# Query and key rows of an attention kernel in transfers of four heads of a row instead of eight

## The chip, the cores and the metric

The kernel runs on one core of a Trainium2 chip. The metric is the device time of one execution in microseconds (us). Matmuls run on TensorE (PE), the other arithmetic on VectorE (DVE), ScalarE (ACT) and GpSimd (POOL); SyncE (SP) computes nothing here, it issues nearly all direct transfers (DMA), in the order of its program, and 16 DMA engines carry them out.

## The reference

32 sequences of 128 tokens with 128 features go through two layers. Layer 0 is a cross-attention with 16 heads of 8 features and then a mixture of 8 experts of which one is chosen; layer 1 is the same attention, masked to be causal, and then 8 experts of which two are chosen. Cut to the parts that the change touches:

```python
x = x + attention0(layernorm(x), ctx, ctx)       # queries from x, keys and values from ctx
x = x + experts0(layernorm(x))
x = x + attention1(layernorm(x), ctx, ctx)       # causal
x = x + experts1(layernorm(x))
# attention: Q, K, V projections + biases, per head of 8 features
scores = einsum('bhqd,bhkd->bhqk', Q, K) / sqrt(8)
out = einsum('bhqk,bhkd->bhqd', softmax(scores), V) @ Wo + bo
```

## The kernel before

The 32 sequences are worked on in eight groups of four (`G = 4`, `GT = 512` tokens). The program has these stages, one after the other, with a barrier of all engines between them except inside the last:

- `prepare`: weights are loaded and turned.
- `project`: for each group n the context rows and the x rows are loaded (lines 406 and 408), x is normalised (statistics on DVE, line 338), both are transposed, and queries of layer 0 and keys of both layers are computed. Each query or key is split into three bf16 parts whose sum is the fp32 value (ACT line 489, DVE 520, ACT 494, POOL 548) and stored to the scratch tensors `q_parts` and `k_parts` in HBM (line 232, three stores of 384 KB for each group, in rows of 1 KB). The part tiles have two buffers, so that the parts of group n wait for the stores of group n-2.
- attention 0: scores from the parts, softmax, product with the values, output projection.
- `experts0`: the layer 0 experts, and the queries of layer 1, which are stored in the same way.
- attention 1 with the layer 1 experts and the final sum behind it, in one block.

In HBM, one row (a part and a feature of the head) of a group holds 16 heads x 512 tokens in bf16. `load_side` (line 228 of the profile) brings one side, query or key, of one group into a tile `qq` or `kk`: partitions 0 to 47 take the first eight heads of each row, partitions 64 to 111 the other eight, 8 heads x 512 tokens x 2 bytes = 8 KB for each partition, side by side. The rows of the three parts go to six slots of eight partitions, some of them twice, in runs of 3, 2 and 1 parts (`RUNS`, `K_RUNS`). One side of a group is so six transfers: three runs x two halves, of 24, 16 and 8 partitions, 192, 128 and 64 KB. `QK_IN` is what the semaphore counts for both sides of a group.

There are three buffers of each tile. The loads stand here in SP's program:

- `project`: after the stores of groups 2, 3 and 4 come both sides of groups 0, 1 and 2 of layer 0 (`early`). The loop body on SP is: load context and x of group n+3, store the parts of group n, and for n = 2, 3, 4 `early(n - 2)`.
- attention 0 and 1: both sides of groups 3 to 7, each when the scores of the group that had the buffer are done (`on_sync`).
- `experts0`: the keys of groups 0, 1, 2 of layer 1 at the start, ahead of the layer 1 weights (lines 1168 to 1172); the queries of these groups each between a store of queries and three fills of `sorted_in` (line 1177).

The readers are TensorE's matmuls of lines 666 (scores) and 687 (scores transposed); scores run three sequences ahead of the rest.

Of the kernel before, what the change touches and what calls it, by code (L numbers as in the profile page):

```python
# [17 lines left out]
DH = D // H  # L18
# [8 lines left out]
RUNS = ((0, 0, 3), (3, 0, 2), (5, 0, 1))  # L27
# [2 lines left out]
HALF = 64  # L30
AHEAD = 3
QK_BUFS = 3
QK_IN = 16 * 2 * 2 * len(RUNS)
STORED = 16
C4 = 4
NC = H // C4
# [12 lines left out]
def earlier(count):  # L49

    return max(count, 0) if isinstance(count, int) else count
# [94 lines left out]
def build(nc, a, out):  # L146
# [16 lines left out]
    with ctx:  # L163
# [57 lines left out]
        def load_side(eng, l, g, side, signal):  # L221

            tile, src, runs = (qq, q_parts[g], RUNS) if side == "q" else (kk, k_parts[l][g], K_RUNS)
            for slot, part, count in runs:
                by_half = src[part:part + count].rearrange("c d (a i) t -> a (c d) i t", a=2)
                for s in range(2):
                    row = s * HALF + slot * DH
                    eng.dma_start(tile[g % QK_BUFS][row:row + count * DH], by_half[s]).then_inc(signal, 16)

        def store_parts(eng, to, tile, signal):  # L230

# [145 lines left out]
        def project():  # L377
# [7 lines left out]
            with ExitStack() as own, nc.Block() as block:  # L385
# [16 lines left out]
                @block.sync  # L402
                def _(sp):
                    def load(g):
                        sp.wait_ge(c_turned, earlier(g.n - 1))
                        sp.dma_start(c_g[g.p][:], rows(a["ctx_1024"], g)).then_inc(c_in[g.p], 16)
                        sp.wait_ge(ln.stats_s, earlier(g.n - 1))
                        sp.dma_start(x_of(g), rows(a["x"], g)).then_inc(x_in[g.p], 16)

                    def store(g):  # L410
                        for i, (_, _, to) in enumerate(items):
                            sp.wait_ge(part2, g.n * 3 + i + 1)
                            store_parts(sp, to[g.n], parts[g.p][i], kq_out[g.p][i])

                    def early(g):
                        for i, side in ((0, "k"), (2, "q")):
                            sp.wait_ge(kq_out[g % 2][i], STORED * (g // 2 + 1))
                            load_side(sp, 0, g, side, early_in[0])

                    load(FIRST)  # L420
                    load(FIRST.after())
                    load(FIRST.after().after())

                    for n in range(NG):
                        if n + 3 < NG:
                            load(Group((n + 3) // 2, (n + 3) % 2))
                        store(Group(n // 2, n % 2))
                        if n >= 2 and n - 2 < QK_BUFS:
                            early(n - 2)
                    for s in kq_out[0] + kq_out[1]:  # L430
                        sp.wait_ge(s, STORED * (NG // 2))
# [133 lines left out]
        def attention(l, own):  # L565
# [66 lines left out]
            def on_sync(sp):  # L632
                def load(g):
                    sp.wait_ge(st_ps, (g - QK_BUFS + 1) * G * PAIRS)
                    for side in "kq":
                        load_side(sp, l, g, side, qk_in[g % QK_BUFS])

                for g in range(QK_BUFS, NG):
                    load(g)
                for g in range(NG - QK_BUFS, NG):  # L640
                    sp.wait_ge(qk_in[g % QK_BUFS], g // QK_BUFS * QK_IN)

            def on_tensor(pe):
# [8 lines left out]
                def scores(n, u):  # L652

                    buf, t = columns(n)
                    if u == 0 and n % G == 0:
                        if n // G < QK_BUFS:
                            pe.wait_ge(early_in[l], QK_BUFS * QK_IN)
                        else:
                            pe.wait_ge(qk_in[buf], n // G // QK_BUFS * QK_IN)
                    pe.wait_ge(max_s, earlier(n * PAIRS + u - (n < AHEAD)))  # L660
# [467 lines left out]
        def experts0():  # L1128
# [9 lines left out]
            with ExitStack() as own, nc.Block() as block:  # L1138
# [19 lines left out]
                def _(sp):  # L1158
# [4 lines left out]
                    def early(g):  # L1163
                        sp.wait_ge(q_out[g % 2], STORED * (g // 2 + 1))
                        load_side(sp, 1, g, "q", early_in[1])
# [581 lines left out]
```

## Time and profile before

| | |
|---|---|
| median of 3 runs | 824.84 us (823.54 to 827.07) |
| the profiled execution's own time | 818.21 us |
| its span, first to last instruction | 816.4 us |
| PE / DVE / ACT / POOL busy | 77% / 59% / 48% / 44% of the span |
| bytes moved by DMA | 87.56 MB in 59708 packets |
| `project` (to the first score matmul) | until 114.6 us of the span |
| attention 0 | 114.6 to about 266 us |
| `experts0` | about 266 to 404 us |
| attention 1 | 404 to about 625 us |
| layer 1 experts, sum | to the end |

Durations of instructions come from the profiled execution, whose own time is 6.6 us below the median of the three runs; its span leaves out 1.8 us around the first and last instruction. In the rows below, SPq is the queue of SP: the time shown there is the time that SP needs to issue a transfer, with what it has to wait for room ahead of it, not the time of the transfer. "DMA share" is the mean busy share of the 16 DMA engines.

### The profile page before, as it was taken

Reading aid. Unit: us, or ns where it says so; the run is one execution under the profiler, and the core shown is the slowest. Engines: PE = TensorE matmul, PEld = TensorE weight load, DVE = VectorE, ACT = ScalarE, POOL = GpSimd, SP = SyncE. Lnnn points to the kernel's source line nnn. Section 1 sums busy time; section 2 is a strip of 40 time slices with the busy share of each in tenths; the row PEclk is TensorE's granted clock in tenths of the full one; section 3 lists DMA queues with packets and bytes.
Section 4 is the critical chain, followed back from the end, with each engine's and each line's share of the span. In section 5 each row is a group of like instructions: output and inputs, shape, how many; then the busy total and the mean of one; then the engine's idle time right before and its main releaser. Section 6 shows DMA issues by size and latency. Waiting matters only on the chain. (4 is left out here: it accounts for less than half of the span.)

```text
span 816.4 us, 22712 instructions
## 1 busy us (share of the span) xinstructions
PE 626.6 (77%) x8205; PEld 478.1 (59%) x8205; DVE 482.4 (59%) x1255; ACT 392.5 (48%) x900; POOL 359.6 (44%) x555
## 2 busy tenths in 40 slices
PE   1574549979998589999389988888740799999980
PEld 1353327757676344544166765666530799999980
DVE  1462356757773367675266789888725355555545
ACT  0684426757776234444135766566730344444440
POOL 5384350101000325352324467777886255555550
PEclk9996768999999699999569999999955799999995
DMA  3389831635400875587604444320011222222218
GB/s 83 113 239 193 208 138 32 111 70 101 87 3 2 137 229 232 172 228 249 255 2 80 79 89 99 76 55 26 25 44 46 54 67 62 65 63 64 68 33 312
DMA packets 59708, 87.56 MB, mean 107 GB/s; under 512 B 8904, under 2 KB 50128, under 8 KB 56528
## 3 DMA queue, kind: packets, MB, share of 16 engines
q1 hardware_dynamic: 51024, 75.03, 35.8%
q0 software_dynamic: 4352, 8.99, 3.5%
q10 hardware_dynamic: 4224, 2.10, 0.9%
q8 instruction: 68, 1.11, 0.6%
q14 instruction: 40, 0.33, 0.1%
HBM read 43.99 MB, written 41.96 MB: 105 GB/s over the span
## 5 line engine op out<-in xcount | busy, mean ns | idle before, releaser
L893 DVE TENSOR_REDUCE nm<-bank 128x8 f32<-128x1024 f32 x128 | 155.8, 1222 | 50.3 <-PE bank L666 48.4
L796 ACT ACTIVATE pr<-bank 128x512 f32<-128x512 f32 x256 | 147.1, 603 | 77.1 <-PE bank L690 74.6
L1515 PE MATMUL bank<-exxt,qq 128*128 128x128 f32 (+1 forms) x864 | 109.1, 277 | 0.9 <-ACT exxt L1553 0.7
L1515 PEld LDWEIGHTS bank<-exxt,qq 128*128 128x128 f32 (+1 forms) x864 | 101.2, 185 | 1.4 <-ACT exxt L1553 1.1
L1062 POOL TENSOR_SCALAR_AFFINE_SELECT pr<-pr 128x1024 f32<-128x1024 f32 x64 | 69.7, 1089 | 64.5 <-ACT pr L796 63.9
L705 PE MATMUL bank<-pr,values 128*9 128x128 f32 x2048 | 82.2, 279 | 3.5 <-POOL pr L1062 2.0
L1489 POOL DMA_INDIRECT results<-exy,exre x72 | 71.4, 991 | 29.7 <-issue 29.4
L687 PE MATMUL bank<-qq,kk 48*128 48x128 bf16 x1024 | 76.7, 223 | 3.8 <-ACT pr L796 2.6
L690 PE MATMUL bank<-mt,pick 64*128 64x128 bf16 x1024 | 76.7, 223 | 0.1
L1337 PE MATMUL bank<-e0ch,expert_w 128*128 128x512 f32 x128 | 70.3, 632 | 6.5 <-DVE e0ch L1259 6.5
L1589 DVE TENSOR_TENSOR exhi<-bank,exsi 128x384 f32<-128x384 f32 x72 | 40.1, 557 | 55.1 <-PE bank L1515 37.6
L666 PE MATMUL bank<-kk,qq 48*128 48x128 bf16 x1024 | 55.2, 232 | 19.2 <-PEq L157 7.9
L1092 POOL DMA_INDIRECT sorted_in<-rrrow,rrpli x64 | 63.4, 991 | 14.2 <-issue 14.2
L1523 PE MATMUL bank<-down_w,exhi 128*128 (+1 forms) x432 | 60.1, 275 | 0.1
L666 PEld LDWEIGHTS bank<-kk,qq 48*128 48x128 bf16 x1024 | 37.9, 101 | 37.8 <-issue 19.4
L1566 ACT ACTIVATE exy<-bank,exsh 128x128 f32<-128x128 f32 x72 | 26.5, 368 | 67.5 <-PE bank L1523 43.4
L1069 POOL CAST mp<-nm 128x16 bf16<-128x16 f32 x32 | 6.3, 198 | 119.1 <-DVE nm L893 116.0
L687 PEld LDWEIGHTS bank<-qq,kk 48*128 48x128 bf16 x1024 | 51.7, 98 | 9.4 <-ACT pr L796 5.0
L705 PEld LDWEIGHTS bank<-pr,values 128*9 128x9 f32 x2048 | 43.9, 91 | 17.7 <-issue 4.1
L1523 PEld LDWEIGHTS bank<-down_w,exhi 128*128 128x128 f32 (+1 forms) x432 | 53.9, 191 | 0.3 <-issue 0.3
L1259 DVE TENSOR_TENSOR e0ch<-bank,e0xt 128x512 f32<-128x512 f32 x64 | 42.8, 680 | 17.5 <-PE bank L1328 17.5
L690 PEld LDWEIGHTS bank<-mt,pick 64*128 64x128 bf16 x1024 | 52.3, 98 | 0.3 <-issue 0.3
(208 smaller groups left out, 1168.2 us busy)
## 6 DMA issues: line engine op xcount, KB each, us to landing
sorted_in<-values SPq DMA_DIRECT2D x25, 715.0 KB, 6.4
k_parts<-pj_parts SPq DMA_DIRECT2D x16, 384.0 KB, 3.8
kk<-k_parts SPq DMA_DIRECT2D x32, 192.0 KB
qq<-q_parts SPq DMA_DIRECT2D x32, 192.0 KB
exx<-sorted_in SPq DMA_DIRECT2D x72, 65.0 KB
kk<-k_parts SPq DMA_DIRECT2D x32, 128.0 KB
qq<-q_parts SPq DMA_DIRECT2D x32, 128.0 KB
q_parts<-pj_parts SPq DMA_DIRECT2D x8, 384.0 KB, 3.9
```

The lines of the kernel that those rows point to most:

```text
L666: mm = pe.matmul(s_pair[:, (a * C4 + j) * T:(a * C4 + j + 1) * T], qq[buf][half(a, PROD), u * C4 + j, t], kk[buf][half(a, PROD), u * C4 + ...
L687: pe.matmul(to[a][:, j * T:(j + 1) * T], kk[buf][half(a, PROD), u * C4 + j, t], qq[buf][half(a, PROD), u * C4 + j, t], start=True, stop=Fa ...
L690: mm = pe.matmul(to[a][:, j * T:(j + 1) * T], pick[half(a, HALF), u * C4 + j, :], max_t[n % 3][half(a, HALF), :], start=False, stop=True, ...
L705: mm = pe.matmul(o_bank[32 * j:32 * j + VW, c * T:(c + 1) * T], values[l][:, n, c % 2 * H2 + c // 2 * C4 + j, :], probs[c][:, j * T:(j + 1 ...
L796: act.activation(probs[c], st_bank[(n * NC + c) % ST][:], ACT.Exp, scale=scale).then_inc(exp_s, 1)
L893: dve.tensor_reduce(neg_max[n % 2][:, u * 2 * C4:(u + 1) * 2 * C4], score_banks(n, u).rearrange("q (h k) -> q h k", k=T), AX_X, ALU.max, n ...
L1062: pool.affine_select(out=probs_pair[u][:], in_=probs_pair[u][:], compare_op=ALU.is_ge, fill=0.0, base=0, pattern=[[0, 2 * C4], [1, T]], ch ...
L1092: pool.indirect_dma_start(sorted_in[:], bass.IndirectOffsetOnAxis(ap=place_i[bt.p][:, k, b:b + 1], axis=0), row[bt.p][:, k, b, :], None).t ...
L1337: pe.matmul(y_bank[:], expert0_w[:, e, :], chosen[e % 2][:], start=(e == 0), stop=(e == E - 1)).then_inc(y_ps, 1)
L1489: pool.indirect_dma_start(results[:], bass.IndirectOffsetOnAxis(ap=result[q.g.p][:, q.b:q.b + 1], axis=0), y_g[q.p][:], None).then_inc(y_o ...
L1515: mm = pe.matmul(to[q.p][0:fn, f * T:(f + 1) * T], own_w[q.p][:, w0 + f0:w0 + f0 + fn], x, start=True, stop=True)
L1523: mm = pe.matmul(y_bank[q.p][:, 0:D], hidden[q.p][0:fn, f * T:(f + 1) * T], down_w[0:fn, bass.ds(e, 1), f, :].rearrange("f e d -> f (e d)" ...
```

## The change

Each half row of eight heads goes in two transfers of four heads. A transfer still has the same 24, 16 or 8 partitions, but takes 4 KB for each partition, so it is 96, 64 or 32 KB. One side of a group is twelve transfers instead of six, and all 32 sides together are 384 transfers instead of 192. The two pieces of a half are issued one behind the other. The bytes, their places in HBM and in SBUF, and the place of the loads in SP's program stay as they are; the count that the readers wait for doubles.

```diff
-QK_IN = 16 * 2 * 2 * len(RUNS)
+QK_IN = 16 * 2 * 2 * 2 * len(RUNS)
...
                 for s in range(2):
                     row = s * HALF + slot * DH
-                    eng.dma_start(tile[g % QK_BUFS][row:row + count * DH], by_half[s]).then_inc(signal, 16)
+                    for u in range(2):
+                        heads = slice(u * C4, (u + 1) * C4)
+                        eng.dma_start(tile[g % QK_BUFS][row:row + count * DH, heads], by_half[s][:, heads]).then_inc(signal, 16)
```

## Rows read from the trace of the kernel before

**Rows 1.** The page: the span, DMA busy tenths in 40 slices, the hardware queue.

```profile
span 816.4 us, 22712 instructions
...
DMA  3389831635400875587604444320011222222218
...
q1 hardware_dynamic: 51024, 75.03, 35.8%
```

**Rows 2.** Waits within 57 to 115 us: engine, line, releaser: total, times, longest.

```profile
DVE pj_ln_stats L338 <- DMA x_res<-x: 25.1, 2, 13.1
```

**Rows 3.** Timeline of SP's queue in `project`: start, us, line, operation.

```profile
55.45 2.50 SPq L228 DMA_DIRECT2D kk<-k_parts  x6
58.00 2.25 SPq L228 DMA_DIRECT2D qq<-q_parts  x6
...
64.16 2.63 SPq L232 DMA_DIRECT2D q_parts<-pj_parts  x1
66.84 5.86 SPq L228 DMA_DIRECT2D kk<-k_parts  x6
72.74 2.53 SPq L228 DMA_DIRECT2D qq<-q_parts  x6
...
75.75 0.51 SPq L408 DMA_DIRECT2D x_res<-x  x1
...
84.94 5.10 SPq L228 DMA_DIRECT2D kk<-k_parts  x6
90.08 2.25 SPq L228 DMA_DIRECT2D qq<-q_parts  x6
93.77 1.49 SPq L232 DMA_DIRECT2D k_parts<-pj_parts  x2
```

**Rows 4.** Timeline of DVE and ACT, same stretch, with the idle time before.

```profile
72.14 0.87 DVE L338 BATCH_NORM_STATS2 pj_ln_stats<-x_res 128x6 f32<-128x128 f32 x4 [12.01 <-DMA x_res<-x]
...
89.68 0.87 DVE L338 BATCH_NORM_STATS2 pj_ln_stats<-x_res 128x6 f32<-128x128 f32 x4 [13.10 <-DMA x_res<-x]
...
105.11 0.69 ACT L489 ACTIVATE pj_parts<-bank,bk 128x512 bf16<-128x512 f32 x1 [0.27 <-DMA k_parts<-pj_parts]
```

**Rows 5.** Windows: stretch, length, engines' busy time, PE clock, DMA share, GB/s.

```profile
54.00:57.00 3.00, 2.80 (x10) 1.61 (x11) 1.24 (x8) 2.28 (x5) 3.00 (x5) 1.00 1.00 349
...
74.40:86.80 12.40, 7.43 (x26) 4.54 (x26) 2.18 (x4) 6.22 (x12) 5.19 (x6) 0.67 0.97 168
...
139.00:152.00 13.00, 12.57 (x272) 9.36 (x274) 9.74 (x16) 9.46 (x23) 1.45 (x7) 1.00 0.69 124
148.00:151.00 3.00, 2.86 (x82) 2.04 (x71) 2.36 (x5) 1.97 (x5) 0.06 (x1) 1.00 0.51 82
799.00:804.00 5.00, 0.00 (x0) 0.00 (x0) 2.79 (x5) 0.00 (x0) 0.00 (x0) 0.50 1.00 397
```

**Rows 6.** A load in attention 0: SP's queue, first reader, DMA packets within 139:152.

```profile
138.38 2.28 SPq L228 DMA_DIRECT2D kk<-k_parts  x6
140.71 2.25 SPq L228 DMA_DIRECT2D qq<-q_parts  x6
...
160.79 0.40 PE L666 MATMUL bank<-kk,qq 48*128 48x128 bf16 x8
...
DMA packets 338, 1.61 MB, mean 124 GB/s; under 512 B 144, under 2 KB 144, under 8 KB 144
```

**Rows 7.** SP's queue in `experts0`: the early loads and what follows them.

```profile
266.52 6.86 SPq L228 DMA_DIRECT2D kk<-k_parts  x18
...
296.39 1.33 SPq L1177 DMA_DIRECT2D sorted_in<-values  x1
...
306.53 0.37 SPq L232 DMA_DIRECT2D q_parts<-e0parts  x1
...
337.54 2.09 SPq L1177 DMA_DIRECT2D sorted_in<-values  x3
348.66 0.38 SPq L232 DMA_DIRECT2D q_parts<-e0parts  x1
```

## Prediction

> **What bounds the kernel now.** I read the page first, then the waits and the timelines of the stages that contain the changed loads, then windows over the DMA queues. On the page, see that DMA is no bound of the whole, 36% of the 16 engines' time, but that its load comes in heaps: nearly all engines are busy in slices 4 and 5 of 40 and again around slice 20 [rows 1]. Those early slices are the last part of `project`. There DVE, which wants the x rows of groups 6 and 7, sits idle twice, 25.1 us together [rows 2], and the timeline shows each time the same cause: the x rows arrive at 72.1 and at 89.7 us, 12.0 and 13.1 us after DVE was ready [rows 4]. SP issues those x rows behind a load of queries and keys [rows 3], and the DMA engines are full all the while, a share of 0.97 from 74.4 to 86.8 us [rows 5]. So for some 35 us this stage goes at the pace of the DMA queues, and three of the changed loads lie inside it.
>
> How the three lie on the path: x of group 6 is queued behind the first load, x of group 7 behind the second. The interval between the two arrivals is 17.5 us [rows 4]. In it move one load, 0.52 MB of context and x, and three stores of 0.39 MB; the last two, 1.70 MB, take 4.9 us at the 349 GB/s that the stores reached [rows 5], which leaves 12.6 us for the load. The third load stands ahead of the stores of group 5, and ACT waited for one of these at 105.1 us for 0.27 us [rows 4], behind 15.4 us of computation since 89.7 us. So a longer first, second or third load each moves the end of the stage one for one; shorter ones count for the first two only, the third has 0.27 us to give.
>
> **A load in detail.** The clean case stands in attention 0. Both sides of a group are 1.57 MB, and with 139 to 152 us at 124 GB/s [rows 5] that is the whole of one load, about 12.5 us. SP needed 4.53 us to issue the twelve transfers, 0.38 us each, and the first reader came 22.4 us after the first issue [rows 6]. Of the packets 144 are small, the marks that engines write at the end of a transfer: twelve for each on the mean [rows 6]. That fits 12, 16 and 8 engines for the transfers of 24, 16 and 8 partitions, and then the busiest eight engines carry 2 + 1 + 1 rows for a half, 16 rows of 8 KB for a load. In the last 3 us about eight engines are still at work, share 0.51, 82 GB/s [rows 5].
>
> An engine at work in the load moves 124 / (0.69 x 16) = 11.2 GB/s, so an 8 KB packet takes 730 ns, and 16 of them 11.7 us, nearly the whole load. Packets can be faster: 1 KB stores run at 349 / 16 = 21.8 GB/s, 47 ns a packet, and loads with 4 KB packets over all partitions at 397 / 16 = 24.8 GB/s, 165 ns [rows 5]. These two give a fixed 8 ns and 0.038 ns a byte, so 323 ns for an 8 KB packet and 330 ns for two of 4 KB. The load therefore takes 12.5 us where its busiest engines would need 16 x 0.323 = 5.2 us. What the other 7.3 us are decides this case: shared bandwidth (stays), a cost for each transfer (doubles), or a handicap of big packets (goes).
>
> The Trainium skill (SBUF — State Buffer, section on the DMA port swizzle) says that a transfer's rate goes by the SBUF ports its partitions reach, that partitions 0 to 63 reach only half of the 16 and that each gives 27.2 GB/s. By that rule the 7.3 us are port sharing: four-head pieces land in the same partitions, and the load keeps its time. The trace agrees in direction: the 128-partition loads reach 397 GB/s, these 124, and 82 at their end [rows 5].
>
> **The change part by part.** (1) SP's issues. A load goes from 12 to 24 issues, 4.5 to 9.1 us at 0.38 us each. In `project` this is covered: SP was at work from 55.4 to 92.3 us, but mostly blocked. The first issue of a load and the stores ahead of it took 2 to 4 us each instead of 0.4 [rows 3]; without the blocking a 17.5 us cycle holds 24 x 0.38 + five others of 0.4 = 11.1 us of issuing, so 6.4 us are spare. The order in the queue is unchanged, and as long as the engines have work queued, a later issue moves nothing. If this cover is gone (engines drained before SP comes), the load takes the pace of the issues. The third load ends its issues at about 97 instead of 92.3 us, and the stores of group 5, issued at 93.8 [rows 3], go out 4 us later, still before the engines finish that load at about 102 us (89.7 us, some 2 us of stores, one load less its first packets on the free engines). Cost 0.
>
> (2) The packets on the busiest engines: 16 more times 8 ns, 0.13 us a load.
>
> (3) The marks: 12 more for each load. Below, nothing: the 4 KB loads ran at share 1.00 through about four ends of transfers [rows 5], so an end leaves hardly a gap. Above, the whole unexplained 7.3 us, 0.61 us for each transfer. I take 0.05 us, near the lower end because that row is of the same queue and direction: 0.6 us a load.
>
> (4) The order within a load: the two pieces of one half follow each other, so engines stay on the same partitions for two packets, and an engine that runs ahead has a smaller packet to run ahead with. Halves overlapping is what keeps more than one set of partitions filling. I bound it by -1 and +2 us and take 0.3 us.
>
> Sum for a load 1.0 us; three on the path of `project`, 3.0 us.
>
> (5) The loads of attention 0 and 1: first issue to first reader is 22.4 us [rows 6], and no less in the nine others. The load occupies 13 of them and would occupy 14, or 20.3 us with the upper bound of (3). Cost 0; TensorE's wait stays met beforehand.
>
> (6) `experts0`. The keys take 36 issues instead of 18, 6.9 us more; the weights and the first fill go out later, the fill done at 297.7 us, and the next store waits for POOL until 306.5 us: 8.8 us of cover [rows 7]. If it were short, the stores of queries would slip, and with their two buffers ACT. Each load of queries adds six issues, 2.4 us, and SP is idle for 9.0 us behind the fills [rows 7]. Cost 0.
>
> **The sum.** 818.2 us for the profiled execution becomes 821.2 us. That execution is 6.6 us below the median of the runs, so for the median 824.8 + 3 = 827.8 us. About 0.5%, 4.1 us, is what a measurement of this kernel can tell from no change.
>
> **Rivals.**
>
> *Port-bound and nothing else.* The 7.3 us are bandwidth of the shared partitions, and marks and packets hide under it: 0 to +1 us, 825 us. For it: the lower rate with fewer partitions. Against: an engine between two packets leaves its share to others only if they share its partitions. Chance 0.17.
>
> *A cost for each transfer.* The excess of 7.3 us comes with the twelve transfers, 0.61 us each, and doubles: up to 7.3 us for each of three loads, +22 us, 847 us; a third of it gives 832 us. It decides from 0.11 us a transfer on, where the sum passes 4 us. For it: the 12.5 us nobody accounts for, and that all transfers but a few are under 200 KB. Against: 4 KB packets at share 1.00 through the ends of transfers [rows 5]. Chance 0.18. The Trainium skill (DMA: Bandwidth & Descriptors, Rules for kernel authors) speaks against this change here: it advises to coalesce and says that under 64 KB one pays mostly overhead; a third of the transfers fall to 32 KB. By its measured table a transfer has a floor of 0.68 us, and 12 of them for each of three loads would be an estimated +24 us. No run here shows that floor between overlapping transfers.
>
> *Big packets were the handicap (the other side).* 4 KB packets go at their own 165 ns even in these partitions, since requests of different engines alternate sooner. Then the engines need 5.3 us, and SP's issues become the pace: the 17.5 us cycle falls to SP's 11.1 us, -6.4 us, and the first load from 12.5 to 9.1 us, -3.4 us; the third gives 0.3 us. Together -10 us, 815 us. It decides where a load gets 2.1 us shorter. For it: 730 ns against 323. Against: the same bytes reach the same partitions. Chance 0.15.
>
> *My forecast*, +1 to +6 us: chance 0.50, of which a third lies above 4.1 us.
>
> **The numbers.** Faster 0.15; same 0.17 + 0.34 = 0.51; slower 0.16 + 0.18 = 0.34. The range 819 to 838 us leaves out the strong half of the gain (0.07) and the costs above 0.36 us a transfer (0.08); my likeliest case alone is 825.8 to 831 us.
>
> **What would show it.** The x rows arrive for DVE at about 73 and 92 us instead of 72.1 and 89.7, and the score matmuls begin at 117.6 instead of 114.6 us. A load alone in attention 0 has 384 packets of 4 KB and 288 marks, lasts 13.5 us, and the DMA share in it stays near 0.69 with the rate near 120 GB/s. SP issues 24 transfers in about 9.1 us. From the first score matmul on nothing is longer. Wrong would be: a load of 9 to 10 us paced by SP's issues (rival with small packets), a load of 15 us or more (cost of transfers), a TensorE wait ahead of a group's first line 666, or a `project` in which DVE no longer waits for x.

## The result, and the profile after

The changed kernel takes 811.68 us (809.55 to 812.49, 4 runs) against 824.19 us (822.76 to 827.07, 4 runs) for the kernel before beside it: a ratio of 0.984, 95% interval 0.981 to 0.987. It is 12.5 us faster where the forecast was 3 us slower, and lies below the forecast range of 819 to 838 us. Some later pairs put the kernel before at 821 to 823 us and the changed one at 811.0 us (ratio 0.9845), so the gain is 11 to 12.5 us. The profiled execution of the changed kernel took 809.55 us, 8.7 us below that of the kernel before.

The page of the changed kernel, which answers to [rows 1]:

```profile
span 807.8 us, 22904 instructions
...
DMA  3379941433301764576503334400011222222209
...
q1 hardware_dynamic: 56400, 75.04, 32.4%
```

Queue q1, which carries SP's transfers, moves the same bytes in 5,376 more packets (3,072 of data, 2,304 marks at the ends of transfers), and yet they take less time of the DMA engines: 32.4% of the span instead of 35.8%.

Where the time went is read from the first instructions of each stage, one profile of each kernel:

| stage, us | before | after |
|---|---|---|
| `project`, to the first score matmul | 114.6 | 113.5 |
| attention 0 | 151.9 | 145.6 |
| `experts0` | 138.3 | 138.5 |
| attention 1, to the first weight matmul of its experts (line 1515) | 234.1 | 230.8 |
| the rest | 177.5 | 179.4 |

So `project`, on which the forecast spent its working, moved by 1 us, attention 0, where it put the cost at nothing, by 6.3 us, and attention 1 by 3.3 us. The 1.9 us in the last row are scatter: over all 18 profiles of this document that stretch takes 177.5 to 179.8 us, whatever the loads.

In `project` the waits (first row, as [rows 2]) and timelines (the others, as [rows 3, 4]) after are:

```profile
DVE pj_ln_stats L340 <- DMA x_res<-x: 24.8, 2, 12.5
```

```profile
55.29 4.91 SPq L230 DMA_DIRECT2D kk<-k_parts  x12
60.24 4.73 SPq L230 DMA_DIRECT2D qq<-q_parts  x12
...
72.31 0.87 DVE L340 BATCH_NORM_STATS2 pj_ln_stats<-x_res 128x6 f32<-128x128 f32 x4 [12.35 <-DMA x_res<-x]
...
89.22 0.87 DVE L340 BATCH_NORM_STATS2 pj_ln_stats<-x_res 128x6 f32<-128x128 f32 x4 [12.47 <-DMA x_res<-x]
```

DVE still waits for x behind the first two loads. The x rows come at 72.3 and 89.2 us instead of 72.1 and 89.7; a load is not longer with twice the transfers, and SP's 24 issues for the first load take 9.6 us, under the cover that was expected.

In attention 0 one wait matters. The kernel before, timeline of TensorE, and two windows (stretch, length, busy of PE, PEld, DVE, ACT, POOL, PE clock, DMA share, GB/s):

```profile
165.91 0.62 PE L705 MATMUL bank<-pr,values 128*9 128x128 f32 x16
170.06 0.40 PE L666 MATMUL bank<-kk,qq 48*128 48x128 bf16 x8 [3.52 <-issue]
```

```profile
166.50:170.00 3.50, 0.04 (x4) 0.00 (x0) 0.58 (x3) 1.10 (x3) 0.00 (x0) 1.00 0.04 7
171.40:174.60 3.20, 3.20 (x44) 2.15 (x42) 1.33 (x3) 1.07 (x3) 0.42 (x2) 0.50 0.02 5
```

```profile
DMA packets 265, 1.12 MB, mean 122 GB/s; under 512 B 128, under 2 KB 128, under 8 KB 128
...
q1 hardware_dynamic: 265, 1.12, 68.3%
```

The changed kernel at the same place of its program, 156.2 to 165.4 us:

```profile
DMA packets 504, 1.15 MB, mean 125 GB/s; under 512 B 230, under 2 KB 230, under 8 KB 502
...
q1 hardware_dynamic: 502, 1.12, 50.4%
q8 instruction: 2, 0.03, 1.5%
```

q8 carries packets of 16 KB. In attention 0 of the kernel before they are 4.1 to 8.5 us apart but for one place: one started at 156.8 us and the next at 167.2 us, just as the load's last packet of data ended; TensorE began again at 170.1 us. After, the largest distance is 7.6 us, and the waits of TensorE in the whole of attention 0 are these:

```profile
PE bank L718 <- ACT ot L803: 1.2, 4, 0.4
PE bank L725 <- DVE on L906: 0.9, 1, 0.9
PE bank L729 <- ACT ont L808: 0.4, 1, 0.4
```

The bytes and the rate are nearly the same, 122 and 125 GB/s; the load's queue holds 50% of the engines' time instead of 68%. That share alone does not decide: in e1 and e5 below the same load holds 64.0 and 66.2%, and TensorE does not idle.

### The profile page after: what moved, and what is told of

It is laid out like the page before. It is cut to its first block, busy times and chain, and to the rows that moved or that the text cites. A ratio compares the mean times of both kernels' runs of the same rounds, so it can differ in the third digit from the quotient of the medians.

```text
span 807.8 us, 22904 instructions
## 1 busy us (share of the span) xinstructions
PE 623.4 (77%) x8205; PEld 475.4 (59%) x8205; DVE 480.5 (59%) x1255; ACT 392.3 (49%) x900; POOL 360.8 (45%) x555
## 3 DMA queue, kind: packets, MB, share of 16 engines
q1 hardware_dynamic: 56400, 75.04, 32.4%
## 4 chain that ended last, share of the span: by engine, by line
PE 28%; DVE 9%; issue 5%; POOL 4%; ACT 2%; DMA 2%; SPq 0%; POOLq 0%; ACTq 0%; DVEq 0%
PE bank L1517 12%; PE bank L1525 6%; DVE nm L895 3%; POOL sorted_in L1094 3%; PE bank L707 2%; PE bank L651 1%; PE bank L689 1%; ACT pr L798 1%; PE bank L1505 1%; POOL pr L1064 1%; PE bank L718 1%; PE bank L668 1%; PE bank L692 1%; PE bank L743 1%; PE bank L729 1%
## 5 line engine op out<-in xcount | busy, mean ns | idle before, releaser
L668 PEld LDWEIGHTS bank<-kk,qq 48*128 48x128 bf16 x1024 | 37.4, 100 | 33.2 <-DVE nm L895 17.3
```

The source lines that it names most:

```text
L668: mm = pe.matmul(s_pair[:, (a * C4 + j) * T:(a * C4 + j + 1) * T], qq[buf][half(a, PROD), u * C4 + j, t], kk[buf][half(a, PROD), u * C4 + ...
```

## The experiments

Theory A: loads that fill the DMA engines hold up the transfers that bring TensorE its instructions (the fetches). Theory B: the early loads on `project`'s path got shorter. The loads that attention 0 and 1 issue for groups 3 to 7 are called reloads below. All were timed with the kernel before on the same chip; "gap" is the largest distance between two packets of q8 in attention 0, "idle" TensorE's longest wait on issue there, both from the one profile, in us. The last column, "stops", is explained below the table.

| run | us | ratio, 95% interval | attention 0 | gap | idle | stops in attention 0 / 1 |
|---|---|---|---|---|---|---|
| before | 821.4 to 822.9 | | 151.9 | 10.4 | 3.5 | 4.8 / 2.7 |
| e1 reloads split | 812.95 | 0.987, 0.983 to 0.991 | 146.3 | 8.0 | none | 0 / 0 |
| e2 early loads split | 820.24 | 0.997, 0.994 to 0.9998 | 152.0 | 12.2 | 4.2 | 4.4 / 2.8 |
| e3 4 KB packets only | 828.47 | 1.005, 1.001 to 1.008 | 154.1 | 12.5 | 4.8 | 7.3 / 3.6 |
| e4 no reloads | 812.12 | 0.985, 0.981 to 0.989 | 145.9 | 7.6 | none | not counted |
| e5 tiny transfers between | 814.27 | 0.990, 0.986 to 0.994 | 146.2 | 7.8 | none | 0 / 0 |
| e6 sides spaced | 816.03 | 0.991, 0.988 to 0.994 | 146.6 | 8.3 | 0.3 | 1.6 / 0.6 |
| e7 changed kernel again | 810.97 | 0.9845, 0.981 to 0.988 | 145.9 | 7.7 | none | 0 / 0 |
| e8 reloads in quarters | 831.86 | 1.011, 1.007 to 1.015 | 168.0 | 11.5 | none | 0 / 0 |
| e9 group 4 only | 819.15 | 0.996, 0.992 to 0.9999 | 146.4 | 8.2 | none | 1.0 / 3.8 |
| e10 attention 1 only | 817.47 | 0.994, 0.991 to 0.997 | 154.0 | 11.2 | 4.5 | 6.6 / 0 |
| e11 early moved, whole | 812.41 | 0.988, 0.982 to 0.994 | 152.4 | 12.3 | 4.5 | 5.2 / 3.3 |
| e12 early moved, split | 809.42 | 0.985, 0.980 to 0.989 | 145.7 | 7.8 | none | 0 / 0 |
| e13 early in attention, whole | 804.83 | 0.979, 0.975 to 0.984 | 155.3 | 9.5 | 2.4 | 2.9 / 2.9 |
| e14 early in attention, split | 795.36 | 0.967, 0.963 to 0.971 | 148.1 | 9.4 | none | 0 / 0 |
| e15 tiny at reloads only | 812.83 | 0.989, 0.985 to 0.993 | 145.5 | 7.8 | none | 0 / 0 |
| e16 group 4 later | 819.51 | 0.997, 0.994 to 1.0002 | 150.7 | 9.2 | 1.1 | 4.3 / 4.4 |

(Attention 0 of e13 and e14 holds a wait for group 1's rows besides, 3.9 and 1.5 us; in e14 the gap of 9.4 us lies around that wait.)

**Are the packets of q8 TensorE's instructions?** Counting in the traces answers it. In all 18 profiles q8 has 68 packets, on the mean 255.4 to 256.7 of TensorE's instructions apart (17,521 in all but e4: matmuls, weight loads and its waits). Number the packets of a trace from k = 0, and compare each run with the changed kernel, instruction by instruction: in nine profiles (the kernel before, e2, e3, e6, e9, e10, e11, e13, e16) TensorE stops for over 0.25 us longer at 52 places of the attention stages that lie exactly 449 + 256 k instructions after its first, and it goes on 1.3 to 1.8 us after packet k has ended. Their sums, in us, are the last column. Nowhere else in these stages does TensorE stop for over 0.9 us longer than in the changed kernel, but for the waits for rows in e8, e13 and e14. So TensorE had used up the instructions before those of packet k, and waited for packet k. (e4 has ten instructions fewer and can't be compared so; TensorE has no wait on issue in its attention 0.)

The stops are there in every stage whose reloads are all whole and issued fast, in attention 0 and in attention 1, and in no stage where all are split, quartered or followed by tiny transfers. In the kernel before they add up to 4.8 us in attention 0; at the lower clock level behind the longest TensorE ran for 3.4 us at half speed. Together that is near the 6.3 us that the stage lost.

**Which loads: e1 and e2.** `load_side` got the number of pieces as an argument; e1 splits the reloads, e2 the others.

```diff
-                        load_side(sp, l, g, side, qk_in[g % QK_BUFS])
+                        load_side(sp, l, g, side, qk_in[g % QK_BUFS], 2)
```

> Only the loads of groups 3 to 7 in the two attention stages go in pieces of four heads; the early loads stay whole. Theory A: the gain of 12.5 us comes from the attention stages, where TensorE stood without instructions while loads of 8 KB packets filled the DMA engines (attention 0 ran 152.0 us before and 145.6 after). It expects nearly all of the gain here: 812 to 815 us, attention 0 about 146 us, no wait of TensorE on issue of over 1 us in it. Theory B: the gain comes from the three early loads that project waits for; it expects 822 to 825 us here. Theory C: it is spread over both by the packet's size; it expects 817 to 820 us.

> The other half: only the early loads (project, and experts0) go in pieces of four heads, those of groups 3 to 7 stay whole. Theory A expects 821 to 825 us, with project about 1 us shorter, as in the changed kernel, and the long TensorE wait on issue in attention 0 still there. Theory B expects 812 to 815 us. If both halves give less than their share, the two act together, by the time at which loads and instruction fetches meet.

The reloads give 9.9 us and the early loads 2.6 us, together the 12.5 us. Theory A has the large part, and e2 keeps the idle spell, at a time just below the 821 to 825 us expected. The small part is barely told from no change by its time, and e2's profile alone does not show its place: `project` ends at 114.3 us, and in the kernel before at 114.6. All profiles together do. With whole early loads in their old place (the kernel before, e1, e4, e6, e8, e9, e10, e15, e16) `project` ends at 114.0 to 117.1 us, 116.0 on the mean; with split ones (the changed kernel twice, e2) at 113.5 to 114.9, 114.3 on the mean. So theory B has a part too, about 1.7 us, and the kernel before was profiled in one of its shorter executions.

**How much the reloads cost: e4.** The reloads and the waits for them are taken out; what is left out is the loading of groups 3 to 7, which compute with old rows.

> Leaves work out: the query and key rows of groups 3 to 7 are never loaded in either layer, and these groups compute with what stands in the buffers. This is the floor for everything that those ten loads do to the attention stages. Theory A (fetches of instructions held up by the loads): attention 0 falls to 145 us or less and the whole to 808 to 812 us; the changed kernel then has got back nearly all that the loads cost. Theory B: attention 0 stays near 152 us and the whole at 822 to 825 us, since the loads are hidden. If it is far below 805 us, the loads cost in another way too, such as bandwidth for other traffic.

812.1 us: the floor. Reloads that no reader ever waited for had cost 10.7 us, and split reloads (e1, 813.0) cost within noise of nothing.

**Packet size alone: e3.** The tiles have two halves with a little padding between them; one transfer then makes two runs of 4 KB for each row.

```diff
-        qq = [sb(f"qq{p}", [128, H2, GT], BF16, attn) for p in range(QK_BUFS)]
+        qq_full = [sb(f"qq{p}", [128, 2, 4 * GT + 2], BF16, attn) for p in range(QK_BUFS)]
...
-                    eng.dma_start(tile[g % QK_BUFS][row:row + count * DH], by_half[s]).then_inc(signal, 16)
+                    eng.dma_start(tile[g % QK_BUFS][row:row + count * DH],
+                                  by_half[s].rearrange("r (u i) t -> r u i t", u=2)).then_inc(signal, 16)
```

> 4 KB packets without more transfers: the query and key tiles get 4 bytes of padding behind the fourth head, so that one transfer of a half row is made of two runs of 4 KB; six transfers for a side as before. If the packet's size does it, the time is that of the changed kernel or less, 808 to 813 us, and a load is shorter than the 11 to 13 us that it keeps in both kernels, since SP issues it in 4.5 us instead of 9.5. If it is the slower pace of issuing that helps (24 issues spread the traffic over more time, so that other traffic gets in between), the time is 820 to 825 us.

828.5 us lies above both branches: a miss for the packet's size, and no gain of any kind. The load of group 4 in e3 has 4 KB packets (the DMA answer for 159 to 173 us; the marks are again 144):

```profile
DMA packets 530, 1.61 MB, mean 115 GB/s; under 512 B 144, under 2 KB 144, under 8 KB 528
...
q1 hardware_dynamic: 528, 1.57, 64.6%
```

and behind it TensorE idles as before:

```profile
PE bank L669 <- issue: 4.8, 1, 4.8
```

The early loads even got longer; DVE has x at 74.0 and 93.3 us. Small packets in large transfers are worse than large ones here.

**Pace alone: e5, e15 and e6.** In e5 and e15 each transfer of eight heads is followed by a tiny one, in e15 for the reloads only; in e6 the query side of a reload is issued two sequences later.

```diff
+                    eng.dma_start(tiny[row:row + count * DH, g % QK_BUFS, 0 if side == "q" else 1],
+                                  by_half[s][:, 0, 0:16]).then_inc(signal, 16)
```

```diff
-                    sp.wait_ge(st_ps, (g - QK_BUFS + 1) * G * PAIRS)
-                    for side in "kq":
+                    for i, side in enumerate("kq"):
+                        sp.wait_ge(st_ps, (g - QK_BUFS + 1) * G * PAIRS + i * 2 * PAIRS)
```

> Eight-head transfers as before, each followed by a tiny transfer of the same rows (32 bytes a row, into a tile that nobody reads): as many issues, marks and as slow an issuing as in the changed kernel, but 16 KB a turn for each engine in the largest transfers as before. If the pace of issuing (12 issues in 4.5 us against 24 in 9.5) is what helps, the time is 810 to 816 us, the early key loads of experts0 take about 16 us instead of 20, and TensorE's long wait on issue in attention 0 is gone. If it is the size of a transfer, the time is 820 to 827 us with that wait still there.

> Eight-head transfers everywhere; only in the loads of groups 3 to 7 is each followed by a tiny one of 32 bytes a row. If the pace of issuing is all, this equals reloads in two pieces, 812 to 814.5 us. If the smaller transfers have a part of their own, it stays between, 815 to 819 us.

> Eight-head transfers as before and no more of them, but for groups 3 to 7 the query side is issued two sequences after the key side, so that a load is two bursts of about 6 us with 2 us between instead of one of 12. If TensorE starves because a fetch of its instructions can wait as long as a burst lasts, this takes the gain of the attention stages without any smaller transfer: 811 to 816 us, no wait on issue of over 1 us in attention 0. If the size of packets or transfers decides, it stays at 821 to 825 us.

e15 at 812.8 us equals e1 at 813.0 us with transfers as large as before. Either way a reload of attention 0 lasts 10.6 to 12.5 us from its first packet to its last, against 10.7 to 12.7 us in the kernel before; e15's queue holds 50.4% of the engines' time in it (the answer for 156.9 to 169.2 us):

```profile
q1 hardware_dynamic: 666, 1.56, 50.4%
q8 instruction: 3, 0.05, 1.9%
```

So for the reloads the slower issuing is enough. e6, with bursts of 6 us instead of 12 and the fast issuing, gains 6.1 us, about two thirds of e1's 9.9. A part of e5's expectation missed: the three key loads at the start of `experts0` took 20.2 us from their first packet to their last, as in the kernel before (20.0), not 16, and x came at 74.1 and 92.2 us. In the early loads pacing gives nothing, only smaller transfers do: the key loads take 16.1 to 18.7 us in the five profiles with split ones (the changed kernel twice, e2, e12, e14). The changed kernel again:

> The changed kernel itself, beside the others on the same chip: 809 to 814 us. A second profile shows whether the stretches without instructions stay away in attention 0: it should run 145 to 147 us from the first score matmul to the first statistics of experts0.

**Too fine: e8.** Reloads in four pieces, 48 issues.

> Early loads whole; the loads of groups 3 to 7 in pieces of two heads, 2 KB packets, 48 issues in about 18 us for a load, of the 22.4 us that there are. If a slower pace is all that is needed and the pieces of four heads have already reached the floor, the time equals that of reloads in two pieces, 811 to 815 us. If smaller pieces still gain, under 810 us. If the load comes too late for the scores, TensorE waits before a group's first line of scores and the time is over 820 us.

The third branch: SP needs 20.6 to 22.7 us to issue a load, not the 18 expected, and the readers wait in attention 0, a wait that no other reload caused:

```profile
PE bank L668 <- DMA qq<-q_parts: 16.4, 5, 6.0
```

**One load: e9 and e16; the other layer: e10.** e9 splits group 4's load of layer 0 alone; e16 leaves it whole and issues it one sequence later; e10 splits the five of attention 1.

> One load of the sixteen is in pieces of four heads, that of group 4 in attention 0, in whose stretch TensorE stood for 3.5 us without instructions before; everything else as before. If such single long gaps between fetches of instructions are what the loads cost attention 0, this one load gives 4 to 5 us, 817 to 819 us against about 822.5, and attention 0 runs 147 to 149 us. If the cost lies in a little contention under every load, it gives a tenth of the gain, about 1 us, 821 to 822 us.

> As before but for one thing: the load of group 4 in attention 0 is issued one sequence (4.2 us) later, of 9 to 15 us that it has to spare. If the long gap between fetches hangs on how this load meets them, attention 0 changes by some us with nothing smaller or slower: either the wait of 3.5 to 4.5 us on issue goes (attention 0 at 147 to 149 us, 817 to 819 us) or it moves to another load (152 us, 822 us). A gap that stays at the same place of TensorE's program would speak against the load as its cause.

> Only the five loads of groups 3 to 7 in attention 1 in pieces of four heads. The profiles show attention 1 some 3.3 us shorter with split reloads (234.1 to about 231 us): expected 818.5 to 820 us, about 3 us below the kernel before. If that part is noise of the clock, 822 us.

In e9 attention 0 is about as short as with all reloads split (146.4 us), and the time falls by 3.1 us, less than the 4 to 5 expected and hardly clear of nothing (the single runs spread from 812.8 to 826.6 us).

In e16 the 4.1 us that one sequence lost in the kernel before shrink to 0.9, and three sequences later another loses 3.2. The stops sit at the same instructions as before, since TensorE can only run dry where a packet's instructions end, but their lengths change: for packets 8 and 10 they were 3.4 and 0.5 us and are now 1.0 and 2.2. The second falls under the load of group 5, which SP issues from 173.2 us on. The profile puts it down to ACT, which had been done for 1.0 us:

```profile
180.86 0.61 ACT L796 ACTIVATE pr<-bank 128x512 f32<-128x512 f32 x1
...
182.43 0.62 PE L705 MATMUL bank<-pr,values 128*9 128x128 f32 x16 [2.09 <-ACT pr L796]
```

So shifting one load trades one stop for another, for 1.9 us that are not clear of nothing.

e10 is worth 4.7 us, more than the 3 expected, and keeps the idle spell of attention 0. Its attention 1 takes 230.6 us, as in the other profiles with split reloads (230.6 to 231.3 us), against 233.2 to 236.5 us in the seven with whole ones issued fast; e6 and e15 lie between, at 232.0.

**The early loads off `project`'s path: e11 to e14.** The load of group 0 goes behind the stores of group 4, those of groups 1 and 2 behind all stores (e11 with whole, e12 with split transfers), or to the start of SP's part of attention 0 (e13, e14), each group with a semaphore of its own.

```diff
-                        if n >= 2 and n - 2 < QK_BUFS:
-                            early(n - 2)
+                        if n == 4:
+                            early(0)
...
+                if l == 0:
+                    for g in (1, 2):
+                        for side in "kq":
+                            load_side(sp, 0, g, side, first_in[g])
                 for g in range(QK_BUFS, NG):
                     load(g)
```

> Eight-head transfers as before, but the early loads are taken out of the way of project: group 0's goes behind the stores of group 4, when no more context or x rows are to come, and those of groups 1 and 2 behind all stores, each with a semaphore of its own. The x rows should arrive without the waits of 12 and 13 us, project end at 98 to 103 us instead of 114.6, and the time fall by 11 to 16 us if nothing else starves. But 25 us of full queues now lie over the start of attention 0: if whole loads starve TensorE of instructions, a wait on issue of several us shows there, and the time falls by 4 to 12 us only: 808 to 820 us.

> The changed kernel with the same move of the early loads. Pieces of four heads leave room for the fetches, so the whole gain of the move should stay: project ends at 98 to 103 us, attention 0 runs 145 to 148 us, 796 to 800 us. If group 1's rows come too late (they are needed 12 us after the start of attention 0, and the load takes 11 to 13 us from shortly before it), TensorE waits up to 4 us for them and the time is 800 to 804 us.

> Eight-head transfers; the early load of group 0 behind the stores of group 4, those of groups 1 and 2 at the start of SP's part of attention 0, so that the barrier does not wait for SP. If the early loads are what project waits for, it ends at 97 to 99 us instead of 114.6. The loads of groups 1 and 2 then fill the queues for 25 us from the start of attention 0: TensorE waits 1 to 4 us for group 1 and some 4 us for instructions. 800 to 808 us.

> The changed kernel with the same move. Project ends at 97 to 99 us; TensorE waits up to 4 us for the rows of group 1, which are issued over 9.5 us, but not for instructions; the rest is as in the changed kernel. 796 to 801 us, and so below both kernels. If the early loads were not what project waited for, it ends at 110 us or more and the time is 808 to 812 us.

e12 missed its 796 to 800 us: x came at 60.3 and 67.4 us, but attention 0 began at 114.2 us, since the barrier behind `project` waits for SP, and SP was issuing (timeline of e12). In e11, with half as many issues, it began at 105.2 us, also later than the 98 to 103 expected.

```profile
93.54 4.93 SPq L231 DMA_DIRECT2D kk<-k_parts  x12
98.51 4.74 SPq L231 DMA_DIRECT2D qq<-q_parts  x12
103.30 4.66 SPq L231 DMA_DIRECT2D kk<-k_parts  x12
108.00 4.67 SPq L231 DMA_DIRECT2D qq<-q_parts  x12
...
114.19 1.04 PE L674 MATMUL bank<-kk,qq 48*128 48x128 bf16 x16 [29.08 <-PEq L157]
```

With the issues inside the next stage (e14) the first score matmul starts at 96.0 us:

```profile
95.81 4.35 SPq L231 DMA_DIRECT2D kk<-k_parts  x11
...
95.99 1.04 PE L676 MATMUL bank<-kk,qq 48*128 48x128 bf16 x16 [10.97 <-PEq L157]
```

and TensorE waits 1.5 us for group 1. 795.4 us is 26 us below the kernel before and 16 us below the changed one. The split is worth 9.5 us here, between e13 and e14 (ratios 0.979 and 0.967), a little less than the 11 to 12.5 us at the old place and more than the 3.0 us between e11 and e12, where the doubled issuing in front of the barrier takes back what the split gives. Some 7 of the 9.5 us lie in attention 0: with whole loads TensorE waits 3.9 us instead of 1.5 for group 1's rows, and stops for 2.9 us.

## Why the prediction was wrong

- *The step that failed* is (5), "the loads of attention 0 and 1 ... Cost 0". It asked when the readers need the rows, and that was right: no reader waited in either kernel. It did not ask who else needs the DMA engines. The covered reloads cost 10.7 us (e4), by holding up the queue of the instructions until TensorE ran out of them: stops of 4.8 us in attention 0, with a spell at the lower clock behind the longest, and of 2.7 us in attention 1. The split gives 9.9 us of it back (e1).
- *What the 7.3 us of a load are.* The forecast called this what decides the case and offered shared bandwidth, a cost for each transfer, big packets. The second is out: twice the transfers leave a load as long (e15, and the changed kernel's), and their marks cost nothing seen. The third is out: e3. In the load of group 4 an 8 KB packet takes 664 ns at the median (kernel before), a 4 KB packet 333 ns when it is issued fast (e3) and 214 ns when it is issued slowly (changed kernel): the time for a byte goes with how much is under way at once and not with the packet's size. That fits the first, shared bandwidth, but where the bandwidth is shared was not measured. With the faster issuing, what is issued sooner only stands in the queues longer. The forecast that the DMA share of a load stays near 0.69 missed: from the first to the last packet of a reload it is 0.65 to 0.74 before and, in four of five reloads, 0.48 to 0.52 after.
- *Steps (2) to (4)*, +1.0 us a load and +3.0 us in `project`: wrong in sign. x of group 7 came 0.5 us sooner and `project` ended 1.1 us sooner; over the profiles named above the means are 90.5 us against 89.6 and 116.0 against 114.3, and e2 gives 2.6 us. The terms were not measured one by one; since (2) and (3) can't be gains, it is left to (4), the order and size of the pieces, which is argued and not shown.
- *Step (1)*, SP's issues under cover: right in `project`, 9.6 us for 24 with 6.4 us to spare in the cycle; in attention 0 they take 9.9 to 12.2 us, which the readers did not feel either. *Step (6)*: right, `experts0` took 138.5 us against 138.3.
- *The early loads lie on `project`'s path*: right. Without them there the stage ends at 96.0 to 97.6 us instead of 114.6 (e13, e14).
- *The rivals.* The one on the other side came nearest to the time, with 815 us, but by luck, on another road: it has SP's issues set the pace of shorter loads in `project`, and no load of `project` became shorter like that. A rule of the Trainium skill was set beside the dearest rival: DMA: Bandwidth & Descriptors, Rules for kernel authors, advises to coalesce and calls transfers under 64 KB mostly overhead. Here a third of the loads' transfers fell to 32 KB and the kernel is 1.6% faster; the measurement decides. (In quarters, with 16 KB for the smallest, it is 1.1% slower, e8.)
- *What the profile had shown beforehand.* The idle spell of 3.5 us stood in the trace of before, in the middle of a stage that the sum passed over since its loads were hidden. The chain of work that ended last did not reach back before 404 us, so that it could not point there.

What is shown and what is not. That q8 carries TensorE's instructions, and that TensorE stopped for want of them, is shown by the count above. The gap alone is a rougher sign: in attention 0 TensorE idles on issue 3.5 us behind a gap of 10.4 us, 4.2 behind 12.2, 4.8 behind 12.5, but not in e8 and e14 with gaps of 11.5 and 9.4 us, where it waited for rows and used up fewer instructions; and attention 1 has a gap of 12 us near its start in every kernel.

Not known is which of the 16 engines carry q8, nor how a fetch came to wait for the whole of group 4's load when others began in the midst of a load. In the kernel before, e2, e3 and e10 the late fetch starts within 0.2 us of the end of the load's last packet of data. The same page of the Trainium skill, section on queues, rings and completion order, says that an engine takes turns between its queues packet by packet, a packet being 9 to 17 descriptors as a rule. If the 8 KB packets of this profile are the page's packets, a fetch would wait for one or a few of 664 ns, and the 10.4 us do not agree; if they are its descriptors, 9 to 17 of them last an estimated 6 to 11 us, and the 10.4 us would be in reach. No run tells the two apart. Open too is why small transfers, and neither pacing nor small packets, shorten the early loads.

## What to carry to other kernels

A transfer that nobody waits for can still cost: beside its readers ask which other queues share the DMA engines, and look for TensorE idle on "issue" during or just after a full load, also where the profile names an engine that had long been done. Cut such a load up, or let the issuing engine spread it over the time that there is, down to the point where the readers begin to wait (e8). Loads of the next stage belong inside that stage's program, ahead of its first reader but not ahead of the barrier, which also waits for the engine that only issues (e12 against e14).

## What the runs showed of the hardware

- q8 brings TensorE its instructions, 256 in each packet of 16 KB. With whole reloads issued fast it went 10.4 to 12.5 us without a packet in attention 0, with idle spells of TensorE of 3.5 to 4.8 us (kernel before, e2, e3, e10, e11); TensorE goes on 1.3 to 1.8 us after the end of the packet that it lacked.
- The load of group 4 took 12.6 us from its first packet to its last when SP issued it in 4.5 us (kernel before) and 13.1 us when SP issued it in 11.5 us (changed kernel); in the middle of it the engines were 68 and 50% busy, at 122 and 125 GB/s.
- Twice the transfers, each of half the size, had no cost that could be seen as long as SP had the time to issue them, 0.4 to 0.5 us each.
- 4 KB runs inside transfers of the old size made the loads of `project` longer: the cycle between the x rows of groups 6 and 7 was 19.3 us (e3), against 16.8 to 18.6 us in the nine profiles with 8 KB runs and 16.8 to 17.3 us in the three with split transfers.
